# Layer 0's attention values in blocks of 128 context rows, dealt to the sequences by their stores

## What is computed

```python
q = (x @ Wq)...; k = (context @ Wk)...; v = (context @ Wv).reshape(B, M, 8, 64).transpose(0, 2, 1, 3)
attn = softmax(einsum('bhnd,bhmd->bhnm', q, k) * scale)
out = einsum('bhnm,bhmd->bhnd', attn, v)
return out.transpose(0, 2, 1, 3).reshape(B, N, INNER) @ Wo + bo
```

## Time and profile before

| | before |
|---|---|
| median of 3 runs | 786.82 us |
| the profiled execution, and its span | 791.3 us, 789.5 us |
| PE busy in the span | 667.8 us, 85% |
| DVE | 575.2 us, 73% |
| ACT | 449.0 us, 57% |
| POOL | 476.2 us, 60% |

### The profile page before, as it was taken

One profiled execution on the slowest core, in us unless ns is written; L12 is line 12 of the kernel. 1 busy time (PEld: TensorE's weight loads), 2 busy tenths in 40 slices (PEclk: granted clock), 3 DMA queues, 4 the chain that ended last, 5 costly groups with the idle time before them and its releaser, 6 DMA issues.

```text
span 789.5 us, 17248 instructions
## 1 busy us (share of the span) xinstructions
PE 667.8 (85%) x4720; PEld 603.6 (76%) x4720; DVE 575.2 (73%) x2005; ACT 449.0 (57%) x1219; POOL 476.2 (60%) x693
## 2 busy tenths in 40 slices
PE   6888988988787879987979898899888876888896
PEld 5667877877676879987968787788778876878785
DVE  3467888788567687898886888987968753735772
ACT  3466766665454656766666786686666553334451
POOL 4125357675457777887573335676566577577771
PEclk9999999998788899999989999999999996999998
DMA  9637556343344334545633443532532023344645
GB/s 262 177 81 191 168 158 173 111 116 108 93 117 132 90 103 116 151 115 139 177 86 99 109 104 67 153 98 56 131 96 74 24 57 88 99 119 122 188 132 177
DMA packets 130990, 95.91 MB, mean 121 GB/s; under 512 B 30504, under 2 KB 119112, under 8 KB 130832
## 3 DMA queue, kind: packets, MB, share of 16 engines
q1 hardware_dynamic: 113200, 69.15, 33.5%
q0 software_dynamic: 9088, 19.68, 7.7%
q10 hardware_dynamic: 8608, 5.99, 2.7%
HBM read 55.09 MB, written 44.10 MB: 126 GB/s over the span
## 4 chain that ended last, share of the span: by engine, by line
PE 36%; DVE 28%; issue 12%; ACT 10%; POOL 7%; DMA 4%; DVEq 1%; SPq 1%; POOLq 0%; ACTq 0%
PE banks L1031 7%; PE banks L895 5%; DVE row_max L1264 4%; DVE prob L1267 3%; PE banks L1050 3%; POOL y_rows L1693 3%; PE banks L775 3%; DMA y_rows<-y_sb,result_at 2%; PE banks L777 2%; PE banks L776 2%; POOL x_rows L1686 2%; PE banks L862 2%; ACT vo L1155 2%; PE banks L839 2%; PE banks L880 2%
## 5 line engine op out<-in xcount | busy, mean ns | idle before, releaser
L1693 POOL DMA_INDIRECT y_rows<-y_sb,result_at x156 | 151.4, 970 | 58.7 <-issue 32.4
L1031 PE MATMUL banks<-xb,up 128*128 128x128 f32 x936 | 142.3, 290 | 17.3 <-DVE hidden L1512 5.1
L1686 POOL DMA_INDIRECT x_rows<-xm,row x128 | 127.5, 996 | 36.0 <-issue 29.9
L1031 PEld LDWEIGHTS banks<-xb,up 128*128 128x128 f32 x936 | 123.2, 200 | 25.7 <-DVE up L1504 9.8
L1050 PE MATMUL banks<-down,hidden 128*128 x624 | 99.6, 284 | 7.9 <-DVE y_sb L1529 7.8
L1648 POOL TENSOR_TENSOR v_flat<-v_raw,row_head 104x64 f32<-104x64 f32 (+1 forms) x128 | 55.8, 463 | 74.7 <-ACT v_raw L1186 74.3
L1050 PEld LDWEIGHTS banks<-down,hidden 128*128 128x128 f32 x624 | 85.2, 198 | 10.9 <-issue 10.6
L1264 DVE TENSOR_REDUCE row_max<-banks 128x8 f32<-128x616 f32 x96 | 75.7, 788 | 21.7 <-PE banks L839 11.6
L895 PE MATMUL banks<-v_flat,prob_t 128*128 128x108 f32 (+2 forms) x640 | 87.7, 286 | 3.2 <-issue 1.5
L895 PEld LDWEIGHTS banks<-v_flat,prob_t 128*128 128x128 f32 (+1 forms) x640 | 80.7, 199 | 11.1 <-ACT prob_t L1170 6.6
L1170 ACT ACTIVATE prob_t<-banks 128x512 f32<-128x512 f32 x192 | 72.7, 432 | 27.8 <-PE banks L862 26.7
(11 more groups left out here) (212 smaller groups left out, 1614.0 us busy)
## 6 DMA issues: line engine op xcount, KB each, us to landing
v_rows<-vo SPq DMA_DIRECT2D x64, 154.0 KB
vo_flat<-v_rows SPq DMA_DIRECT2D x32, 256.0 KB
x_norm<-x_rows SPq DMA_DIRECT2D x86, 72.0 KB
x_far<-x_rows SPq DMA_DIRECT2D x70, 72.0 KB
gathered<-y_rows ACTq DMA_DIRECT2D x32, 128.0 KB
q_rows<-up_raw SPq DMA_DIRECT2D x8, 512.0 KB, 2.8
q_even<-q_rows SPq DMA_DIRECT2D x12, 256.0 KB
q_odd<-q_rows SPq DMA_DIRECT2D x12, 256.0 KB
```

The costliest lines, as they stand in the source:

```text
L1031: done = pe.matmul(banks[:, UP_BANK[i % 2], part * P:(part + 1) * P], block_w[:, i % WR, part // 2, part % 2 * P:(part % 2 + 1) * P], xb[: ...
L1686: pool.indirect_dma_start(out=x_rows[i // HG][:, :], out_offset=bass.IndirectOffsetOnAxis(ap=row[:, n, c:c + 1], axis=0), in_=xm[:, i % 2, ...
L1693: pool.indirect_dma_start(out=y_rows[k][:, :], out_offset=bass.IndirectOffsetOnAxis(ap=result_at[:, i % (2 * YR):i % (2 * YR) + 1], axis=0 ...
```

## The change

The values are no longer made for each sequence (77 rows) but for blocks of 128 rows of the flat context: 20 blocks, of which the last has 32 rows. `v0` tasks are now (block, half). The new function `value_halves` says which halves stand in which step; the first of a step takes the place of the old first half, the rest that of the old second half. The store of a half becomes one DMA for each sequence that the block covers (`value_pieces`), `v_rows` gets a place for each of the 32 sequences, `vo0` has 128 partitions, and the semaphore of the stores is split by half. ACT's copy of a half waits only for the stores of the same half of the blocks before. The load of a sequence's values waits for all stores issued before it.

```diff
+def value_halves():
+    begun, out = 2, []
+    for u in range(NSEQ):
+        last = ((min(u + 2, NSEQ) * NKEY) - 1) // P
+        n = min(max(2 * (last + 1), (5 * (u + 1) + 13) // 4), 2 * CTX_BLOCKS)
+        out.append([("v0", k // 2, k % 2) for k in range(begun, n)])
+        begun = n
+    return out
...
-            step += [("v0_load", u)] + [("v0", u + 1, 0)][:u + 1 < NSEQ] + [("divide0", u)] + more[1]
+            step += [("v0_load", u)] + values[u][:1] + [("divide0", u)] + more[1]
...
-            step += [("v0", u + 1, 1)][:u + 1 < NSEQ] + [("bias0", u)] + more[2]
+            step += values[u][1:] + [("bias0", u)] + more[2]
...
-    v_rows = [nc.dram_tensor(f"v_rows{i}", [UNIT_ROWS, D], F32, kind="Internal").ap() for i in (0, 1)]
+    v_rows = nc.dram_tensor("v_rows", [NSEQ, UNIT_ROWS, D], F32, kind="Internal").ap()
...
+        def value_pieces(n):
+
+            rows = range(n * P, min((n + 1) * P, CTX_ROWS))
+            starts = [r for r in rows if r == rows[0] or r % NKEY == 0]
+            return [(r // NKEY, r % NKEY, r - n * P, min(NKEY - r % NKEY, rows[-1] + 1 - r)) for r in starts]
...
                 elif t[0] == "v0":
-                    b, h = t[1:]
-                    half_rows = v_rows[b % 2][h * (UNIT_ROWS // 2):(h + 1) * (UNIT_ROWS // 2), :]
-                    w.wait_ge("v0", 2 * b + h + 1)
-                    w.wait_ge(f"v0_in{b % 2}", 32 * (b // 2))
-                    sync.dma_start(half_rows.rearrange("(a n) d -> n a d", n=NKEY), vo0[:, h, :, :]).then_inc(sem("v0_out"), 16)
+                    n, h = t[1:]
+                    w.wait_ge("v0", 2 * n + h + 1)
+                    for b, key, first, count in value_pieces(n):
+                        to = v_rows[b].rearrange("(a n) d -> n a d", n=NKEY)[key:key + count, 4 * h:4 * h + 4, :]
+                        sync.dma_start(to, vo0[first:first + count, h, :, :]).then_inc(sem(f"v0_out{h}"), 16)
+                        values_out[h] += 16
                 elif t[0] == "v0_load":
...
-                    w.wait_ge("v0_out", 32 * (b + 1))
+                    for h in (0, 1):
+                        w.wait_ge(f"v0_out{h}", values_out[h])
...
-                    done = three_pass(banks[0:NKEY, V_BANK, :], ctx_th[:, c0:c0 + NKEY], ctx_tl[:, c0:c0 + NKEY], four(wvo_h), four(wvo_l))
+                    done = three_pass(banks[0:cols.stop - cols.start, V_BANK, :], ctx_th[:, cols], ctx_tl[:, cols], four(wvo_h), four(wvo_l))
...
-                    w.wait_ge("v0_mm", 2 * b + h + 1)
-                    w.wait_ge("v0_out", 32 * b)
-                    act.activation(vo0[:, h, :, :].rearrange("p h d -> p (h d)"), banks[0:NKEY, V_BANK, :],
+                    n, h = t[1:]
+                    rows = min(P, CTX_ROWS - n * P)
+                    w.wait_ge("v0_mm", 2 * n + h + 1)
+                    w.wait_ge(f"v0_out{h}", 16 * sum(len(value_pieces(m)) for m in range(n)))
+                    act.activation(vo0[0:rows, h, :, :].rearrange("p h d -> p (h d)"), banks[0:rows, V_BANK, :],
                                    ACT.Copy).then_inc(sem("v0"))
```

More of the change, by code:

```diff
@@ L122, in route_tasks @@
     return {u: sorted(step, key=lambda t: layer == 1 and t[0] == "scatter") for u, step in at.items()}
+def value_halves():
[6 more added lines that the diff above has]
+    return out
 def attention0_steps(tasks):
+    values = value_halves()
     background = [("ctx", i) for i in range(2, CTX_SETS)] + [("weights1",), ("tables", 0)]
@@ L519, in flamingo_two_layers @@
         k0_t = layer0_only.enter_context(nc.sbuf_tensor("k0_t", [P, 2, 2, GS, NH0, NKEY], F32R))
-        vo0 = layer0_only.enter_context(nc.sbuf_tensor("vo0", [NKEY, 2, NH0 // 2, D], F32))
+        vo0 = layer0_only.enter_context(nc.sbuf_tensor("vo0", [P, 2, NH0 // 2, D], F32))
         vo_flat = layer0_only.enter_context(nc.sbuf_tensor("vo_flat", [P, 2, CHUNKS, D], F32))
@@ L649, in _ @@
                 sync.dma_start(x_rows[k][NEXP * REGION:, :], empty_rows[NEXP * P:, :]).then_inc(sem("spare"), 16)
+            values_out = [0, 0]
             def row_register(entry, most):
@@ L676, in _ @@
                         w.wait_ge("split_mm", place["k0", NG - 1, NH0 - 1] + 1)
-                        w.wait_ge("v0_mm", 2 * NSEQ)
+                        w.wait_ge("v0_mm", 2 * CTX_BLOCKS)
                         load(up1[:, e, 0, :], a["L1_ffn_w1"][e], "up1")
@@ L692, in _ @@
                     full = CHUNKS - 1
-                    w.wait_ge("v0_out", 32 * (b + 1))
+                    for h in (0, 1):
+                        w.wait_ge(f"v0_out{h}", values_out[h])
                     w.wait_ge("pv", b - 1)
-                    sync.dma_start(vo_flat[:, b % 2, 0:full, :], v_rows[b % 2][0:full * P, :].rearrange("(c p) d -> p c d", p=P)).then_inc(sem(f"v0_in{b % 2}"), 16)
-                    sync.dma_start(vo_flat[0:chunk_rows[full], b % 2, full, :], v_rows[b % 2][full * P:, :]).then_inc(sem(f"v0_in{b % 2}"), 16)
+                    sync.dma_start(vo_flat[:, b % 2, 0:full, :], v_rows[b][0:full * P, :].rearrange("(c p) d -> p c d", p=P)).then_inc(sem(f"v0_in{b % 2}"), 16)
+                    sync.dma_start(vo_flat[0:chunk_rows[full], b % 2, full, :], v_rows[b][full * P:, :]).then_inc(sem(f"v0_in{b % 2}"), 16)
                 elif t[0] == "fetch":
@@ L783, in split_task @@
                     w.wait_ge("ident", 2)
-                    w.wait_ge(f"in_ctx{t[1]}", 16)
+                    w.wait_ge(f"in_ctx{t[1]}", 32 if t[1] == CTX_SETS - 1 else 16)
                     last = min(4 * t[1] + 4, CTX_BLOCKS)
@@ L787, in split_task @@
                         rows = min(P, CTX_ROWS - j * P)
-                        if j == FULL_BLOCKS:
-                            w.wait_ge("in_ctx_tail", 16)
                         c = (j - 4 * t[1]) * P
@@ L922, in _ @@
                 elif kind == "v0":
-                    b, h = t[1:]
-                    c0 = b * NKEY
+                    n, h = t[1:]
+                    cols = slice(n * P, min((n + 1) * P, CTX_ROWS))
                     four = lambda v: v[:, 4 * h:4 * h + 4, :].rearrange("p h d -> p (h d)")
-                    w.wait_ge("v0", 2 * b + h)
-                    w.wait_ge("split_lo", place["ctx", (c0 + NKEY - 1) // (4 * P)] + 1)
+                    w.wait_ge("v0", 2 * n + h)
+                    w.wait_ge("split_lo", place["ctx", n // 4] + 1)
                     w.wait_ge("split_lo", place["wvo", 1] + 1)
-                    done = three_pass(banks[0:NKEY, V_BANK, :], ctx_th[:, c0:c0 + NKEY], ctx_tl[:, c0:c0 + NKEY], four(wvo_h), four(wvo_l))
+                    done = three_pass(banks[0:cols.stop - cols.start, V_BANK, :], ctx_th[:, cols], ctx_tl[:, cols], four(wvo_h), four(wvo_l))
                     done.then_inc(sem("v0_mm"))
@@ L1041, in _ @@
                         w.wait_ge("x_attn", NSEQ)
-                        w.wait_ge("v0", 2 * NSEQ)
+                        w.wait_ge("v0", 2 * CTX_BLOCKS)
                     else:
@@ L1085, in _ @@
                 load(ctx_stage[:, first:last, :], ctx_flat[first * P:last * P, :].rearrange("(n p) d -> p n d", p=P), f"ctx{i}")
-            load(ctx_stage[0:CTX_TAIL, FULL_BLOCKS, :], ctx_flat[FULL_BLOCKS * P:, :], "ctx_tail")
+            load(ctx_stage[0:CTX_TAIL, FULL_BLOCKS, :], ctx_flat[FULL_BLOCKS * P:, :], f"ctx{CTX_SETS - 1}")
             load(gates_raw[:, 0:2], a["g_xattn"].partition_broadcast(P), "gates")
```

## The result

The change makes the kernel slower: 824.14 us (median of 4 runs, 821.61 to 826.79) against 786.32 us for the kernel before in the same rounds, 37.8 us more. The forecast was 767 us.

A forecast was written before the change was run, and what follows sets the result against it. The prediction took layer 0's attention as a pipeline whose bound changes between PE and DVE. Two accounts, 17.4 and 22.8 us, gave 20 us off the 786.82 us median: 767.0 us, range 756 to 780.

The forecast's parts named there:

- What bounds the stage, and what is removed: Layer 0's attention: in-order engines with a changing bound; 24 fewer value groups, 18.7 us of PE and 14.1 us of ACT.
- What each remaining group costs: Value groups with 128 columns instead of 77: nothing taken; at most 4.7 us if the longer weight loads were bare.
- Stores: SP's queue in layer 0's attention: 102 stores instead of 64, 10.8 us more issue, taken as nothing.
- The cover of 7 us: Load of a sequence's values: issued 11 us before use, transfer 3.0 to 4.0 us, so up to 7 us delay is covered.
- The sign that I had named: Ahead of the products with the loaded values (L880): a wait for those values there would show the prediction wrong.
- The moved waits: ACT's copy of a half waits only for that half's stores of the block before: 3.6 us gained.
- The sum: Layer 0's attention: two overlapping accounts, 17.4 and 22.8 us; the middle, 20 us, was taken as the gain.
- (b): Account by pauses in layer 0's attention: 9.4 us PE work, 9.8 us pauses, 3.6 us store wait; together 22.8 us.
- Account (a): Account by the chain: 39% of 35.3 us of value products and copies, 13.8 us, plus 3.6 us store wait: 17.4 us.
- Nothing: Rival, chance 0.04: scattered stores or a late load eat the gain; time within 0.3% of before.
- DVE takes over: Rival, chance 0.17: DVE is already late, so only 4.5 us of scores' waits and 3.6 us of stores go: 779 us.
- The case that ends slower: Clock rival, chance 0.07: idler PE drops to half rate; six more such stretches cost 24 us, giving 791 us.

The follow-up runs named there:

- the split kernel: Changed kernel with pieces of over 16 rows lacking a divisor from 9 to 16 stored as two DMAs: 772.98 us against 788.32, ratio 0.9824 to the kernel before.
- The run with two buffers: Changed kernel, pieces unsplit, with two buffers for each half in vo0 by turns: 819.05 against 787.98 us for the kernel before, ratio 1.0399.

## Why the prediction was wrong

*What bounds the stage, and what is removed:* right. 40 copies of 597 ns (median), ACT 14.5 us less; with the stores mended PE's busy time in the stage fell from 181.72 to 164.79 us, the 16 to 19 us expected.

*What each remaining group costs:* right, by the split kernel, whose clock is that of the kernel before: weight loads of 191 ns in the median against 148, the first matmul of a group 510 ns in the mean against 490, the second 395 in the median against 392, ACT's copy 586 in the mean.

*Stores: this is the step that failed.* I priced a store by its issue (0.284 us) and took its transfer to be that of the 77-row store, 3.0 to 4.0 us, whatever the piece. Stores with a piece of 47, 53, 71 or 73 rows took 7.2 to 11.9 us in the chain, with one DMA engine at work where nothing else was under way. Instead of nothing, the stores cost the steps 50 us (250.5 against 200.45 with the pieces split). The rows that I had could not show it, because all stores of the kernel before had 77 rows; of the Trainium skill's rules I weighed the clock's alone, and not the one on divisors named above. I put the chance of harm from stores at 0.04.

*The cover of 7 us:* wrong too, and of itself. I counted from the load's issue to its use. But the load waits for all stores, and the later stores stand behind that wait, so one late store holds up the next one's issue (167.84, then 168.78 us), and the 10 us come twice. The run with two buffers shows the harm on SyncE's queue without that of the copy's wait. The sign that I had named, a wait for loaded values ahead of the products, is plain there (38.4 us) and hardly seen in the kernel after itself (at most 2.5 us ahead of L903), where ACT's copy is late first.

*The moved waits:* ACT's wait for stores went from 3.6 to 64.1 us instead of to nothing. With split pieces it is 5.1 us in 2 waits around 71 to 80 us, where the table loads fill SyncE's queue. So the 3.6 us that I credited did not come back in the split kernel either.

*The sum:* with the stores mended the kernel gains 1.8%, 13.9 us, and its steps shrink by 12.8 us, against my 20. That is inside the 13 to 27 us of the forecast, at its low end, so the mechanism of the gain holds and its size was too large. The oversized term is (b), the pauses. PE's waits for value copies did go, and more of them than I had counted: 1.9 us in the steps are left of 21.7. But part of that time came back as waits of PE for DVE and ACT:

```profile
PE banks L1026 <- DVE k_t L1312: 8.8, 4, 3.1
...
PE banks L911 <- ACT prob_t L1202: 7.3, 4, 3.7
```

Neither is among PE's waits before. (Of the 7.3 us, 3.6 lie within the steps.) Account (a), 17.4 us less the 3.6 of the store wait, gives 13.8 us, close to what was measured. As it leaves out both the pauses that went and the waits that came, this may be luck.

*The rivals:* none was the right one. "Nothing" had the right place, the stores, with a price that could not reach the other side of zero. "DVE takes over" fits the mended kernel in part, and its forecast held for the one with no value work. The case that ends slower did come, but not by the way that I gave it: the clock did fall, to 0.83 in the stage, but with the waits for stores, since in the split kernel, with the same products, it is 0.94.

## What to carry to other kernels

Before a DMA is cut by the data's own boundaries, list the row counts that come out: a count with no good divisor up to 16 can take two to three times as long as one a few rows longer (71 or 73 rows against 77). Split it at a multiple of 16, or choose the block so that all pieces share a factor; both versions here beat both kernels, the split one with 773 against 788 us, the one with blocks of 112 rows by 0.8%. And a wait for "everything issued so far" on the queue that issues the next stores makes one slow transfer pay twice.

## What the runs showed of the hardware

- A store of 71 or 73 rows of 4 x 512 bytes keeps one of the 16 DMA engines busy: the DMA share is 0.07, at 22 GB/s. Two such stores of 71 rows, one behind the other, take 15.8 us. 128 stores of 33 and 44 rows, with the same bytes as 64 of 77, cost the kernel nothing (ratio 1.0018).
- The issue of a store right behind such a one is held up on SyncE's queue: 5.4 us and more for 6 rows behind 71, and up to 7.7 us in the kernel after, where the median issue takes 0.37 us.
- DVE's subtraction and row sum over 616 elements take 1.31 us instead of 0.80 when one operand has a stride of 8 elements (32 bytes); POOL's division, with the same stride, takes 1.50 instead of 1.22 us.
- The kernel before took 847 us on one chip and 786 to 788 us on the others. The split kernel, profiled on both sides of this gap (834 and 771 us), has layer 0's steps in 201.3 and 200.5 us and layer 1's attention in 227 and 226 us. What was longer on the slow chip lies between the two attentions (190 against 156 us) and behind the second (178 against 152 us), in the experts' phases. Why is not shown.
